# Single-head cross attention: one folded projection Wq·Wkᵀ in place of two, and context rows loaded one tile ahead

## The chip, the cores and the metric

One core of a Trainium2 chip runs the whole kernel. The metric is the device time of one execution in microseconds (us), lower is better. The kernel before took 2476.36 us (median of three runs, 2470.38 to 2479.93).

## The reference

The input x is 32 sequences of 32 tokens with 512 numbers each (1024 tokens in all), and ctx is 32 sequences of 257 rows with 512 numbers. Two layers of cross attention, self attention and a mixture of experts follow each other. Only the first block of layer 0 is touched:

```python
q = layernorm(x) @ Wq + bq          # (32, 32, 512)
k = ctx @ Wk + bk                   # (32, 257, 512)
v = ctx @ Wv + bv
sim  = einsum('bid,bjd->bij', q, k) * 512 ** -0.5
attn = softmax(sim)
x = x + einsum('bij,bjd->bid', attn, v)
```

The kernel never forms k or v. It uses q·(ctx Wk + bk)ᵀ = (q Wkᵀ)·ctxᵀ + q·bk. The row vector q Wkᵀ is called qp here, and q·bk, one number for each token, is the shift. The values are taken in the same way: attn·ctx first, then times Wv.

## The kernel before, in words

A product that needs full precision is done in three TensorE passes (`mm3`, L132 to L136): both operands are split into a high part, which the fast matmul type holds exactly, and a low part, and high·high, high·low and low·high are added in PSUM. ScalarE makes the high part, VectorE or GpSimd subtracts it from the original for the low part.

Work is cut into blocks (`with nc.Block()`), in which every engine has a program of its own. Engines wait for each other by semaphores inside a block, and all engines meet at its end. All large loads are issued by SyncE (SP) in the order of its program: an instruction that waits holds back every load behind it.

Around the change there are these blocks, in order:

1. **Opening** (L143): SP loads x (2 MB) and waits for it. GpSimd makes an identity and two masks.
2. **Layer norm** (`layer_norm("na")`, L186): statistics of eight tiles of 128 tokens (L221, L224), normalised rows (L248), transposes (L304), high and low parts xh (L280) and xl (L253). Beside it SP loads Wq, Wkᵀ and Wv (L321), and ScalarE and GpSimd split Wq (L326, L332).
3. **Projections** (L374): for each half of the tokens (512) four q jobs of 12 matmuls (x by Wq), whose bias ScalarE adds (L397) and whose low part VectorE makes (L415), then four k jobs of 12 matmuls (q by Wkᵀ, copied out at L418), then 32 matmuls of 2 columns (L450) for the shift. SP loads the three biases and the first transposed context, Wkᵀ and Wv are split.
4. **Attention loop** (L474): eight tiles of 128 tokens, which are four sequences each. TensorE's order is written out by hand. In one turn it runs `scores(n+1)` (L614, needs the transposed context `ct` of tile n+1), `turn_p(n)` (L623), `turn_a(n-1)` (L646), `p_ctx(n)` (L632 and L636, needs the context rows `cn` and `cl` of tile n) and `values(n-1)` (L134 to L136). There is one set of four `ct` buffers and one set of four `cn` buffers. So `ct` of a tile can be loaded only when the scores of the tile before are done, and `cn` only when `p_ctx` of the tile before is done.

Semaphore `s_sc` counts finished sequences of scores and starts with a credit of 8. `s_pv` counts finished sequences of p_ctx and starts with a credit of 4. The two load helpers wait like this before, and the SP loop calls them so:

```python
load_turned(n): eng.wait_ge(s_sc, SEQ * n + (SEQ + 1 + j))   # sequence j of scores(n-1) done
load_rows(n):   eng.wait_ge(s_pv, SEQ * n + SEQ)             # p_ctx(n-1) done
with eng.Fori(0, NT - 1) as n:
    load_turned(eng, n + 1)
    load_rows(n)
load_rows(NT - 1)
```

Of the kernel before, what the change touches and what calls it, by code (L numbers as in the profile page):

```python
# [16 lines left out]
F32 = mybir.dt.float32  # L17
# [71 lines left out]
def build(nc, d, out):  # L89
    with ExitStack() as ctx:  # L90
# [50 lines left out]

        s_x, s_id = sem("x_loaded"), sem("ident_made")
        with nc.Block() as block:  # L143
            @block.sync
            def _(eng):
                eng.dma_start(x[:], d["x"].rearrange("(t p) d -> p t d", p=P)).then_inc(s_x, 16)
                eng.wait_ge(s_x, 16)

            @block.gpsimd
            def _(eng):  # L150
                pool.memset(ident[:], 0.0).then_inc(s_id, 1)
                pool.memset(epst[:], LN_EPS)
                plain = Area(fa, F_SIZE).take(P)
                pool.memset(plain, 1.0).then_inc(s_id, 1)
                eng.wait_ge(s_id, 2)
                pool.affine_select(out=ident[:], in_=ident[:], compare_op=ALU.not_equal, fill=1.0,
                                   base=0, pattern=[[-1, P]], channel_multiplier=1)
                pool.tensor_copy(ones[:], plain)

                pool.affine_select(out=earlier[:], in_=plain, compare_op=ALU.is_gt, fill=0.0,  # L160
                                   base=0, pattern=[[1, P]], channel_multiplier=-1)
# [178 lines left out]
        def cross_one_head():  # L340
            scale = float(D) ** -0.5
            f, r = Area(fa, F_SIZE), Area(ra, R_SIZE)
            qp, bv, bk, bq, shift = f.take(DC, T), f.take(D), f.take(DC), f.take(DC), f.take(NT)
            f2 = f.at

            staging = [f.take(DC, D) for _ in range(3)]
            ct = [f.take(DC, S) for _ in range(SEQ)]
            f3 = f.at
            wv = r.take(DC, D), r.take(DC, D)
            bk_parts = r.take(DC, 2)  # L350
            r2 = r.at
            wq, wk = (r.take(DC, D), r.take(DC, D)), (r.take(DC, D), r.take(DC, D))
            q = [r.take(DC, HALF) for _ in range(2)]
# [4 lines left out]
            s_sc, s_bk = sem("xa_scores"), sem("xa_bk_split")  # L358

            def load_turned(eng, n):  # L360
                for j in range(SEQ):
# [5 lines left out]
            layer_norm("na", ahead=((load, high, low), (0, 1, 2), (0,)))  # L367
            s_b, s_mm, s_hi, s_out = sem("xa_biases"), sem("xa_product"), sem("xa_high"), sem("xa_taken")
# [3 lines left out]
            NB = 4  # L372

            with nc.Block() as block:  # L374
                @block.sync
                def _(eng):
# [3 lines left out]
                    load_turned(eng, 0)  # L380

                @block.gpsimd
                def _(eng):
                    low(eng, (1, 2))

                @block.scalar
                def _(eng):
                    high(eng, (1, 2))
                    eng.wait_ge(s_b, 48)
                    for j, (h, kind, c) in enumerate(jobs):  # L390
                        if kind != "q":
                            continue
                        eng.wait_ge(s_mm, j + 1)
                        if h:

                            eng.wait_ge(s_mm, len(jobs) // 2)
                        act.activation(q[0][:, c, :], banks[:, j % NB, :], ACT.Identity,  # L397
                                       bias=bq[:, c:c + 1]).then_inc(s_hi, 1)

                @block.vector  # L400
                def _(eng):
                    eng.wait_ge(s_b, 48)
                    eng.wait_ge(s_b, 48)
                    dve.tensor_copy(bk_parts[:, :, 0], bk).then_inc(s_bk, 1)
                    eng.wait_ge(s_bk, 1)
                    dve.tensor_tensor(bk_parts[:, :, 1], bk, bk_parts[:, :, 0].bitcast(F32),
                                      ALU.subtract).then_inc(s_bk, 1)
                    highs = 0
                    for j, (h, kind, c) in enumerate(jobs):
                        bank = banks[:, j % NB, :]  # L410
                        eng.wait_ge(s_mm, j + 1)
                        if kind == "q":
                            highs += 1
                            eng.wait_ge(s_hi, highs)
                            ins = dve.scalar_tensor_tensor(q[1][:, c, :], bank, bq[:, c:c + 1],  # L415
                                                           q[0][:, c, :].bitcast(F32), ALU.add, ALU.subtract)
                        elif kind == "k":
                            ins = dve.tensor_copy(qp[:, c, h * HALF:(h + 1) * HALF], bank)  # L418
                        else:
                            ins = dve.reduce_sum(shift[:, 4 * h:4 * h + 4],  # L420
                                                 bank[:, 0:8].rearrange("p (t k) -> p t k", k=2), AX_X)
                        ins.then_inc(s_out, 1)

                @block.tensor
                def _(eng):
                    for j, (h, kind, c) in enumerate(jobs):
# [5 lines left out]
                        if kind == "q":  # L432
                            eng.wait_ge(s_w[0], 1)
                            for k in range(DC):
                                ins = mm3(bank, wq[0][:, k, cols], wq[1][:, k, cols], xh[:, k, tok],
                                          xl[:, k, tok], k == 0, k == DC - 1)
                        elif kind == "k":
                            eng.wait_ge(s_w[1], 1)

                            eng.wait_ge(s_out, j - c)  # L440
                            for k in range(DC):
                                ins = mm3(bank, wk[0][:, k, cols], wk[1][:, k, cols], q[0][:, k, :],
                                          q[1][:, k, :], k == 0, k == DC - 1)
                        else:

                            eng.wait_ge(s_bk, 2)
                            for t in range(4):
                                for k in range(DC):
                                    for part in range(2):
                                        ins = pe.matmul(bank[:, 2 * t:2 * t + 2], q[part][:, k, t * P:(t + 1) * P],  # L450
                                                        bk_parts[:, k, :], start=(k + part == 0),
                                                        stop=(k == DC - 1 and part == 1))
# [3 lines left out]
            f = Area(fa, F_SIZE, f2)  # L456
            cn = [f.take(2, D) for _ in range(SEQ)]
            cl = f.take(D)
            f = Area(fa, F_SIZE, f3)
            r = Area(ra, R_SIZE, r2)  # L460
            qg = [f.take(DC, P) for _ in range(2)]
# [6 lines left out]
            s_ctx = [sem(f"xa_ctx{j}") for j in range(SEQ)]  # L468
            s_passed, s_cl, s_own, s_last = (sem(f"xa_{n}") for n in ("passed", "last_rows", "own", "p_last"))
            (s_qg, s_bias, s_exp, s_tp, s_pt, s_pv, s_a, s_at, s_ah, s_al, s_o, s_x, s_links) = (  # L470
                sem(f"xa_{n}") for n in ("q_tile", "bias", "exp", "p_turned", "p_kept", "pv", "a_kept",
                                         "a_turned", "a_high", "a_low", "out", "x_added", "links"))

            with nc.Block() as block:  # L474
                @block.sync
                def _(eng):
                    def load_rows(n):

                        eng.wait_ge(s_pv, SEQ * n + SEQ)
                        eng.dma_start(cl[0:SEQ, :], d["ctxLast"][bass.ds(SEQ * n, SEQ), :]).then_inc(s_cl, 16)  # L480
                        for j in range(SEQ):

                            eng.wait_ge(s_pv, SEQ * n + j + 1)
                            eng.dma_start(cn[j], d["ctx"][SEQ * n + j, 0:2 * P, :]
                                          .rearrange("(k p) e -> p k e", p=P)).then_inc(s_ctx[j], 16)
# [1604 lines left out]
def layouts(i):  # L2090
# [4 lines left out]
    def units(up1, up2, down):  # L2095
# [14 lines left out]
        "L0_xattn_WkT": t(i["L0_xattn_Wk"]),  # L2110
        "L0_attn_w_qkvT": t(i["L0_attn_w_qkv"]),
# [11 lines left out]
    for name in ("L0_xattn_Wq", "L0_xattn_bq", "L0_xattn_bk", "L0_xattn_Wv", "L0_xattn_bv", "L0_attn_ln_gamma",  # L2123
# [21 lines left out]
```

## Time and profile before

| what | value |
|---|---|
| timed runs, median (lowest to highest) | 2476.36 us (2470.38 to 2479.93) |
| profiled execution, span from the first to the last instruction | 2457.6 us |
| TensorE busy (matmul) | 2120.9 us, 86% |
| VectorE, ScalarE, GpSimd busy | 46%, 37%, 39% |
| mean granted TensorE clock | 0.922 |
| all transfers | 298.99 MB, mean 122 GB/s |

The profiled execution was listed with its span alone; the median of the timed runs lies 18.8 us above that span, which is taken as what lies around it.

In the views below PE is TensorE's matmul, PEld its weight load, DVE VectorE, ACT ScalarE, POOL GpSimd, SPq and PEq are the instruction queues of SyncE and TensorE. L12 is line 12 of the kernel. A row of the timeline has the start in us, the busy us, then engine, line, operation, output<-input, the count, and in brackets the idle time before it with what released it. A row of the windows has the stretch, its length, busy us and instruction count of each engine, the granted TensorE clock (1.00 is full speed), the busy share of the DMA engines and the GB/s moved.

### The profile page before, as it was taken

Reading aid. Unit: us, or ns where it says so; the run is one execution under the profiler, and the core shown is the slowest. Engines: PE = TensorE matmul, PEld = TensorE weight load, DVE = VectorE, ACT = ScalarE, POOL = GpSimd, SP = SyncE. Lnnn points to the kernel's source line nnn. Section 1 sums busy time; section 2 is a strip of 40 time slices with the busy share of each in tenths; the row PEclk is TensorE's granted clock in tenths of the full one; section 3 lists DMA queues with packets and bytes.
Section 4 is the critical chain, followed back from the end, with each engine's and each line's share of the span. In section 5 each row is a group of like instructions: output and inputs, shape, how many; then the busy total and the mean of one; then the engine's idle time right before and its main releaser. Section 6 shows DMA issues by size and latency. Waiting matters only on the chain. (4 is left out here: it accounts for less than half of the span.)

```text
span 2457.6 us, 37707 instructions
## 1 busy us (share of the span) xinstructions
PE 2120.9 (86%) x13252; PEld 1820.9 (74%) x13252; DVE 1130.6 (46%) x2057; ACT 897.9 (37%) x1479; POOL 950.9 (39%) x641
## 2 busy tenths in 40 slices
PE   6895888837999975999999999986765999999994
PEld 5543766637999963788888888865544999999993
DVE  4145463765555565232233222348664445544542
ACT  2112121215666642223232323223222555555551
POOL 2002312005777773232223222213212666666654
PEclk9996999958999987999999999968886999999997
DMA  3483000016888883011001100010003566656653
GB/s 124 169 313 115 18 23 29 1 35 245 274 283 276 282 277 128 18 30 33 26 26 28 33 26 26 18 48 5 22 6 142 200 217 213 209 199 219 214 192 124
DMA packets 102450, 298.99 MB, mean 122 GB/s; under 512 B 10912, under 2 KB 27936, under 8 KB 102336
## 3 DMA queue, kind: packets, MB, share of 16 engines
q1 hardware_dynamic: 76928, 232.88, 28.3%
q0 software_dynamic: 11840, 38.81, 5.2%
q10 hardware_dynamic: 13600, 26.22, 2.8%
q8 instruction: 51, 0.84, 0.1%
q14 instruction: 31, 0.25, 0.0%
HBM read 265.10 MB, written 32.77 MB: 121 GB/s over the span
## 5 line engine op out<-in xcount | busy, mean ns | idle before, releaser
L134 PE MATMUL banks<-ra 128*128 128x256 f32 (+3 forms) x3004 | 982.9, 327 | 55.9 <-DVE x L1040 24.7
L135 PE MATMUL banks<-ra 128*128 128x256 f32 (+3 forms) x3004 | 967.4, 322 | 0.0
L136 PE MATMUL banks<-ra 128*128 128x256 f32 (+3 forms) x3004 | 964.0, 321 | 0.0
L134 PEld LDWEIGHTS banks<-ra 128*128 128x128 f32 (+1 forms) x3004 | 577.9, 193 | 119.5 <-issue 39.5
L136 PEld LDWEIGHTS banks<-ra 128*128 128x128 f32 (+1 forms) x3004 | 577.7, 192 | 43.7
L135 PEld LDWEIGHTS banks<-ra 128*128 128x128 f32 (+1 forms) x3004 | 579.4, 193 | 36.1
L1475 POOL TENSOR_TENSOR ra<-fa,ra 128x1024 fp32r<-128x1024 f32 x187 | 445.9, 2385 | 235.3 <-ACT ra L1508 234.4
L1508 ACT ACTIVATE ra<-fa 128x1536 fp32r<-128x1536 f32 x190 | 281.5, 1482 | 85.1 <-DMA fa<-in_L_units 67.9
L1592 DVE TENSOR_TENSOR ra<-fa,ra 128x256 fp32r<-128x256 f32 x190 | 162.7, 856 | 92.0 <-ACT ra L1532 92.0
L332 POOL TENSOR_TENSOR ra<-fa,ra 128x2048 fp32r<-128x2048 f32 (+2 forms) x22 | 85.7, 3905 | 284.3 <-ACT ra L326 277.4
L1567 DVE TENSOR_TENSOR ra<-fa,ra 128x512 fp32r<-128x512 f32 x190 | 133.6, 703 | 114.9 <-ACT ra L1508 108.2
L1824 POOL TENSOR_TENSOR fa<-fa 128x1028 f32<-128x1028 f32 x32 | 60.9, 1902 | 284.0 <-DVE fa L1916 284.0
L1907 DVE TENSOR_TENSOR fa<-banks,fa 128x512 f32<-128x512 f32 x64 | 44.3, 692 | 269.6 <-PE banks L136 269.6
L1812 POOL TENSOR_TENSOR ra<-fa,ra 128x1032 fp32r<-128x1032 f32 x32 | 77.0, 2405 | 168.7 <-ACT ra L1843 168.7
L1590 DVE TENSOR_TENSOR fa<-banks,fa 128x256 f32<-128x256 f32 x190 | 80.5, 424 | 124.4 <-ACT fa L1528 124.4
L304 PE MATMUL banks<-ident,na 128*128 128x128 f32 x192 | 40.9, 384 | 109.9 <-DVE na L248 86.6
L1528 ACT ACTIVATE fa<-banks 128x256 f32<-128x256 f32 x190 | 72.7, 383 | 165.5 <-PE banks L136 165.4
L1470 POOL DMA_INDIRECT fa<-normed_scratch,fa x100 | 100.1, 1001 | 55.9 <-POOL fa L1465 40.7
L304 PEld LDWEIGHTS banks<-ident,na 128*128 128x128 f32 x192 | 33.4, 203 | 118.0 <-DVE na L248 89.9
L1532 ACT ACTIVATE ra<-fa 128x256 fp32r<-128x256 f32 x190 | 79.4, 418 | 112.5 <-DVE fa L1590 112.5
L1851 ACT ACTIVATE fa<-banks,fa 128x258 f32<-128x258 f32 x128 | 60.9, 477 | 148.5 <-PE banks L136 148.5
L1574 DVE TENSOR_TENSOR ra<-banks,ra 128x512 fp32r<-128x512 f32 x100 | 64.4, 687 | 108.9 <-ACT ra L1512 108.8
(222 smaller groups left out, 2608.4 us busy)
## 6 DMA issues: line engine op xcount, KB each, us to landing
fa<-in_L_units SPq DMA_DIRECT2D x190, 768.0 KB, 4.3
fa<-in_ctxT SPq DMA_DIRECT2D x64, 514.0 KB, 5.3
ea_y_scratch<-fa ACTq DMA_DIRECT2D x35, 512.0 KB, 4.5
fa<-in_ctx SPq DMA_DIRECT2D x32, 512.0 KB, 5.3
eb_y_scratch<-fa ACTq DMA_DIRECT2D x15, 512.0 KB, 3.7
fa<-in_L_attn_w_qkvT SPq DMA_DIRECT2D x6, 1024.0 KB, 6.2
normed_scratch<-na SPq DMA_DIRECT2D x16, 256.0 KB, 2.1
x<-in_x SPq DMA_DIRECT2D x1, 2048.0 KB, 8.2
```

Of the source, the lines that this page charges most:

```text
L134: pe.matmul(psum, lh, rh, start=first, stop=False)
L135: pe.matmul(psum, lh, rl, start=False, stop=False)
L136: return pe.matmul(psum, ll, rh, start=False, stop=last)
L332: pool.tensor_tensor(lo, staging[k % slots], hi.bitcast(F32), ALU.subtract).then_inc(s_w[k], 1)
L1470: pool.indirect_dma_start(xt[u][:, s, :], None, normed_dram, bass.IndirectOffsetOnAxis(ap=ids[u].bitcast(U32)[:, s:s + 1], axis=0)).then_i ...
L1475: pool.tensor_tensor(wl[b][:, 0:2, :], st[b][:, 0:2, :], wh[b][:, 0:2, :].bitcast(F32), ALU.subtract).then_inc(s_wp, 1)
L1508: act.activation(wh[b], st[b], ACT.Copy).then_inc(s_wh, 1)
L1532: act.activation(hh_[b], hf[b], ACT.Copy).then_inc(s_hh, 1)
L1567: dve.tensor_tensor(wl[b][:, 2, :], st[b][:, 2, :], wh[b][:, 2, :].bitcast(F32), ALU.subtract).then_inc(s_wd, 1)
L1590: dve.tensor_tensor(hf[b], banks[:, HB + b, CAP:2 * CAP], sg[b], ALU.mult).then_inc(s_hf, 1)
L1592: dve.tensor_tensor(hl[b], hf[b], hh_[b].bitcast(F32), ALU.subtract).then_inc(s_hl, 1)
L1812: pool.tensor_tensor(cx[u][1], stg[u], cx[u][0].bitcast(F32), ALU.subtract).then_inc(s_cl, 1)
```

## The change

The kernel forms M = Wq·Wkᵀ on the chip and multiplies x by M, so that q is never formed. The biases come in as vectors: u = Wq·bk gives the shift x·u, bq·Wkᵀ (`through_k`) is added to qp, and bq·bk (`both`) to the shift. The opening now loads Wqᵀ, Wkᵀ, x, Wv and the first transposed context, splits both weights, runs 48 matmuls for M and 72 matmuls of 2 columns for the bias terms, and takes the statistics of x. The layer norm block loads the first context rows and splits Wv. The projection block keeps the k jobs and the shift. The SP loop of the attention block calls the same two helpers, but with `load_rows(n + 1)`. `layer_norm`, `split_programs` and TensorE's program in the attention loop are the same text.

```diff
-        s_x, s_id = sem("x_loaded"), sem("ident_made")
-        with nc.Block() as block:
-            @block.sync
-            def _(eng):
-                eng.dma_start(x[:], d["x"].rearrange("(t p) d -> p t d", p=P)).then_inc(s_x, 16)
-                eng.wait_ge(s_x, 16)
...
-            load, high, low, s_w = split_programs("xa", [
-                (*wq, columns(d["L0_xattn_Wq"])), (*wk, columns(d["L0_xattn_WkT"])),
-                (*wv, columns(d["L0_xattn_Wv"]))], staging)
+            cn = [Area(fa, F_SIZE, f2 + 2 * D * j).take(2, D) for j in range(SEQ)]
+            load, high, low, s_w = split_programs("xa", [(*wv, columns(d["L0_xattn_Wv"]))], staging[2:])
...
-            layer_norm("na", ahead=((load, high, low), (0, 1, 2), (0,)))
+            def load_rows(eng, n):
+                if not (isinstance(n, int) and n == 0):
+                    eng.wait_ge(s_pv, SEQ * n + SEQ)
+                eng.dma_start(cl[0:SEQ, :], d["ctxLast"][bass.ds(SEQ * n, SEQ), :]).then_inc(s_cl, 16)
+                for j in range(SEQ):
+                    if not (isinstance(n, int) and n == 0):
+                        eng.wait_ge(s_pv, SEQ * n + j + 1)
+                    eng.dma_start(cn[j], d["ctx"][SEQ * n + j, 0:2 * P, :]
+                                  .rearrange("(k p) e -> p k e", p=P)).then_inc(s_ctx[j], 16)
             with nc.Block() as block:
                 @block.sync
+                def _(eng):
+                    eng.dma_start(staging[0], columns(d["L0_xattn_WqT"])).then_inc(s_wq, 16)
+                    eng.dma_start(staging[1], columns(d["L0_xattn_WkT"])).then_inc(s_wk, 16)
+                    eng.dma_start(x[:], d["x"].rearrange("(t p) d -> p t d", p=P)).then_inc(s_x, 16)
+                    load(eng)
+                    load_turned(eng, 0)
+                    eng.wait_ge(s_x, 16)
+                    eng.wait_ge(s_b, 48)
+                @block.gpsimd
...
+                    eng.wait_ge(s_wh, 1)
+                    pool.tensor_tensor(wq[1], staging[0], wq[0].bitcast(F32), ALU.subtract).then_inc(s_wlo, 1)
+                @block.scalar
                 def _(eng):
                     eng.dma_start(bq, d["L0_xattn_bq"]).then_inc(s_b, 16)
                     eng.dma_start(bk, d["L0_xattn_bk"]).then_inc(s_b, 16)
                     eng.dma_start(bv, d["L0_xattn_bv"].partition_broadcast(P)).then_inc(s_b, 16)
...
+                    eng.wait_ge(s_wq, 16)
+                    act.activation(wq[0], staging[0], ACT.Copy).then_inc(s_wh, 1)
+                    eng.wait_ge(s_wk, 16)
+                    act.activation(wk[0], staging[1], ACT.Copy).then_inc(s_wh, 1)
+                    for c in range(DC):
+                        eng.wait_ge(s_fold, c + 1)
+                        act.activation(m[0][:, c, :], banks[:, c, :], ACT.Copy).then_inc(s_mh, 1)
+                @block.vector
+                def _(eng):
...
+                    eng.wait_ge(s_wh, 2)
+                    dve.tensor_tensor(wk[1], staging[1], wk[0].bitcast(F32), ALU.subtract).then_inc(s_wlo, 1)
+                    eng.wait_ge(s_x, 16)
+                    for t in range(NT):
+                        dve.bn_stats(stats[:, t, :], x[:, t, :])
+                    for c in range(DC):
+                        eng.wait_ge(s_mh, c + 1)
+                        dve.tensor_tensor(m[1][:, c, :], banks[:, c, :], m[0][:, c, :].bitcast(F32),
+                                          ALU.subtract).then_inc(s_ml, 1)
...
+                @block.tensor
+                def _(eng):
+                    eng.wait_ge(s_wlo, 2)
+                    for c in range(DC):
+                        cols = slice(c * P, (c + 1) * P)
+                        for k in range(DC):
+                            ins = mm3(banks[:, c, :], wq[0][:, k, cols], wq[1][:, k, cols], wk[0][:, k, :], wk[1][:, k, :],
+                                      k == 0, k == DC - 1)
+                        ins.then_inc(s_fold, 1)
+                    eng.wait_ge(s_parts, 1)
+                    for w, parts, bank in ((wq, bk_parts, 4), (wk, bq_parts, 5)):
+                        for c in range(DC):
+                            for k in range(DC):
+                                for part in range(2):
+                                    ins = pe.matmul(banks[:, bank, 2 * c:2 * c + 2], w[part][:, k, c * P:(c + 1) * P],
+                                                    parts[:, k, :], start=k + part == 0, stop=k == DC - 1 and part == 1)
...
+                    for k in range(DC):
+                        for part in range(2):
+                            ins = pe.matmul(banks[:, 6, 0:2], bq_wide[part][:, k, :], bk_parts[:, k, :], start=k + part == 0,
+                                            stop=k == DC - 1 and part == 1)
+            made.add("statistics")
+            layer_norm("na", ahead=((load_first_rows, high, low), (0,), (0,)))
-            jobs = [(h, kind, c) for h in range(NHALF) for kind, c in
-                    [("q", c) for c in range(DC)] + [("k", c) for c in range(DC)] + [("shift", 0)]]
+            jobs = [(h, kind, c) for h in range(NHALF) for kind, c in [("k", c) for c in range(DC)] + [("shift", 0)]]
...
-                        elif kind == "k":
-                            ins = dve.tensor_copy(qp[:, c, h * HALF:(h + 1) * HALF], bank)
+                        if kind == "k":
+                            ins = dve.tensor_scalar(qp[:, c, h * HALF:(h + 1) * HALF], bank, through_k[:, c:c + 1], None,
+                                                    ALU.add)
...
-                                ins = mm3(bank, wk[0][:, k, cols], wk[1][:, k, cols], q[0][:, k, :],
-                                          q[1][:, k, :], k == 0, k == DC - 1)
+                                ins = mm3(bank, m[0][:, k, cols], m[1][:, k, cols], xh[:, k, tok], xl[:, k, tok],
+                                          k == 0, k == DC - 1)
...
                     with eng.Fori(0, NT - 1) as n:
                         load_turned(eng, n + 1)
-                        load_rows(n)
-                    load_rows(NT - 1)
+                        load_rows(eng, n + 1)
```

## Rows read from the trace of the kernel before

**Rows 1.** The page: span, busy time, and the KB of one transposed load.

```profile
span 2457.6 us, 37707 instructions
PE 2120.9 (86%) x13252; PEld 1820.9 (74%) x13252; DVE 1130.6 (46%) x2057; ACT 897.9 (37%) x1479; POOL 950.9 (39%) x641
...
fa<-in_ctxT SPq DMA_DIRECT2D x64, 514.0 KB, 5.3
```

**Rows 2.** Timeline, one steady turn of the attention loop: TensorE and SP's queue.

```profile
136.47 4.63 PE L614 MATMUL banks<-fa 128*32 128x257 f32 x32
...
138.57 3.03 SPq L365 DMA_DIRECT2D fa<-in_ctxT  x4
...
142.81 1.11 PE L632 MATMUL banks<-fa 4*128 4x512 f32 x2 [0.81 <-DVE fa L557]
...
143.86 1.94 PE L636 MATMUL banks<-fa 128*32 128x512 f32 x16
...
146.65 2.18 SPq L484 DMA_DIRECT2D fa<-in_ctx  x4
148.73 4.63 PE L614 MATMUL banks<-fa 128*32 128x257 f32 x32
```

**Rows 3.** Timeline: where p_ctx(0) and p_ctx(6) end, the loop's first and seventh.

```profile
106.86 3.20 PE L636 MATMUL banks<-fa 128*32 128x512 f32 x16
...
180.53 1.94 PE L636 MATMUL banks<-fa 128*32 128x512 f32 x16
```

**Rows 4.** Windows of 1 us around the end of a p_ctx at 145.8.

```profile
145.00:146.00 1.00, 1.00 (x9) 0.27 (x2) 0.02 (x1) 0.00 (x0) 0.00 (x0) 1.00 1.02 415
...
148.00:149.00 1.00, 1.00 (x6) 0.48 (x5) 0.16 (x1) 0.00 (x0) 0.00 (x0) 1.00 0.51 129
149.00:150.00 1.00, 1.00 (x8) 0.58 (x8) 0.86 (x2) 0.00 (x0) 0.00 (x0) 1.00 1.04 401
```

**Rows 5.** L484, 180 to 195 us: last rows issued at 184.4; issue to landing.

```profile
L484 SPq DMA_DIRECT2D fa<-in_ctx x4: 378/468/468, 183.0 to 184.4; - x4
...
DMA to landing us min/median/max: 3.9/5.2/6.3
```

**Rows 6.** Timeline: stretches of TensorE at the lower clock, and the projections' marks.

```profile
27.70 0.76 PE L134 MATMUL banks<-xh,ra 128*128 128x512 f32 x1 [4.64 <-PEq L186]
...
30.83 0.46 PE L135 MATMUL banks<-xl,ra 128*128 128x512 f32 x1
...
42.38 0.47 PE L134 MATMUL banks<-ra 128*128 128x512 f32 x1 [1.73 <-DVE ra L415]
...
53.34 3.63 PE L450 MATMUL banks<-ra 128*128 128x2 f32 x32
...
71.58 0.47 PE L134 MATMUL banks<-ra 128*128 128x512 f32 x1 [1.72 <-DVE ra L415]
...
88.00 6.72 PE L614 MATMUL banks<-fa 128*32 128x257 f32 x32 [1.34 <-ACT fa L508]
```

**Rows 7.** Windows of 1 us: in p_ctx(0), and in the next layer norm.

```profile
108.00:109.00 1.00, 1.00 (x8) 0.22 (x4) 0.00 (x0) 0.00 (x0) 0.00 (x0) 0.50 1.01 403
...
223.00:224.00 1.00, 0.61 (x3) 0.64 (x4) 1.00 (x2) 0.13 (x1) 1.00 (x1) 0.50 0.00 0
```

**Rows 8.** Timeline, opening and layer norm.

```profile
14.68 0.64 DVE L224 BATCH_NORM_AGGREGATE moments<-stats 128x2 f32<-128x6 f32 x8
...
18.44 0.69 DVE L253 TENSOR_TENSOR xl<-banks,xh 128x512 fp32r<-128x512 f32 x1
...
20.86 1.91 ACT L326 ACTIVATE ra<-fa 128x2048 fp32r<-128x2048 f32 x1
...
22.85 4.51 POOL L332 TENSOR_TENSOR ra<-fa,ra 128x2048 fp32r<-128x2048 f32 x1 [20.66 <-ACT ra L326]
...
34.37 4.62 DVE L406 TENSOR_TENSOR ra<-fa,ra 128x4 fp32r<-128x4 f32 x1
```

**Rows 9.** L321, first 27 us: landing of Wq, Wkᵀ and Wv after issue.

```profile
DMA to landing us min/median/max: 5.4/7.9/9.9
```

More of the change, by code:

```diff
@@ L343, in cross_one_head @@
             qp, bv, bk, bq, shift = f.take(DC, T), f.take(D), f.take(DC), f.take(DC), f.take(NT)
+            through_k, both, plain = f.take(DC), f.take(2), f.take(P)
             f2 = f.at
@@ L347, in cross_one_head @@
             ct = [f.take(DC, S) for _ in range(SEQ)]
+            cl = f.take(D)
             f3 = f.at
             wv = r.take(DC, D), r.take(DC, D)
-            bk_parts = r.take(DC, 2)
+            m = r.take(DC, D), r.take(DC, D)
+            bk_parts, bq_parts, u_parts = r.take(DC, 2), r.take(DC, 2), r.take(DC, 2)
             r2 = r.at
             wq, wk = (r.take(DC, D), r.take(DC, D)), (r.take(DC, D), r.take(DC, D))
-            q = [r.take(DC, HALF) for _ in range(2)]
-            load, high, low, s_w = split_programs("xa", [
-                (*wq, columns(d["L0_xattn_Wq"])), (*wk, columns(d["L0_xattn_WkT"])),
-                (*wv, columns(d["L0_xattn_Wv"]))], staging)
+            bq_wide = r.take(DC, P), r.take(DC, P)
+            cn = [Area(fa, F_SIZE, f2 + 2 * D * j).take(2, D) for j in range(SEQ)]
+            load, high, low, s_w = split_programs("xa", [(*wv, columns(d["L0_xattn_Wv"]))], staging[2:])
             s_ctxT = [sem(f"xa_ctxT{j}") for j in range(SEQ)]
-            s_sc, s_bk = sem("xa_scores"), sem("xa_bk_split")
+            s_ctx = [sem(f"xa_ctx{j}") for j in range(SEQ)]
+            s_cl, s_sc, s_pv = sem("xa_last_rows"), sem("xa_scores"), sem("xa_pv")
+            s_x, s_id, s_b, s_wq, s_wk = (sem(f"xa_{n}") for n in ("x_loaded", "ident_made", "biases", "wq_loaded", "wk_loaded"))
+            s_wh, s_wlo, s_parts, s_fold, s_mh, s_ml, s_u, s_links0 = (
+                sem(f"xa_{n}") for n in ("folded_high", "folded_low", "bias_parts", "folded", "m_high", "m_low", "u_split",
+                                         "links0"))
             def load_turned(eng, n):
@@ L379, in _ @@
                     eng.dma_start(bv, d["L0_xattn_bv"].partition_broadcast(P)).then_inc(s_b, 16)
[L380 to L398, printed above, removed]
+                    eng.wait_ge(s_wq, 16)
@@ new lines, in _ @@
+                    dve.tensor_tensor(bk_parts[:, :, 1], bk, bk_parts[:, :, 0].bitcast(F32), ALU.subtract)
+                    links.link(dve.tensor_tensor(bq_parts[:, :, 1], bq, bq_parts[:, :, 0].bitcast(F32), ALU.subtract))
+                    for part in range(2):
+                        ins = dve.tensor_copy(bq_wide[part], bq_parts[:, :, part].bitcast(F32).unsqueeze(2)
+                                              .to_broadcast([P, DC, P]))
+                    ins.then_inc(s_parts, 1)
@@ new lines, in _ @@
+                    dve.reduce_sum(through_k, banks[:, 5, 0:2 * DC].rearrange("p (c k) -> p c k", k=2), AX_X)
+                    dve.reduce_sum(both[:, 0:1], banks[:, 6, 0:2], AX_X)
+                @block.tensor
[14 more added lines that the diff above has]
+                                                    parts[:, k, :], start=k + part == 0, stop=k == DC - 1 and part == 1)
+                        if bank == 4:
+                            ins.then_inc(s_fold, 1)
+                    for k in range(DC):
+                        for part in range(2):
+                            ins = pe.matmul(banks[:, 6, 0:2], bq_wide[part][:, k, :], bk_parts[:, k, :], start=k + part == 0,
+                                            stop=k == DC - 1 and part == 1)
+                    ins.then_inc(s_fold, 1)
@@ L409, in _, with load_first_rows @@
+            made.add("statistics")
+            def load_first_rows(eng, _):
+                load_rows(eng, 0)
+            layer_norm("na", ahead=((load_first_rows, high, low), (0,), (0,)))
+            s_mm, s_out = sem("xa_product"), sem("xa_taken")
+            jobs = [(h, kind, c) for h in range(NHALF) for kind, c in [("k", c) for c in range(DC)] + [("shift", 0)]]
+            NB = 4
+            with nc.Block() as block:
+                @block.vector
+                def _(eng):
                     for j, (h, kind, c) in enumerate(jobs):
@@ L467, in cross_one_head @@
             at = [(r.take(DC, P), r.take(DC, P)) for _ in range(2)]
[L468 to L471, printed above, removed]
+            s_passed, s_own, s_last = (sem(f"xa_{n}") for n in ("passed", "own", "p_last"))
+            (s_qg, s_bias, s_exp, s_tp, s_pt, s_a, s_at, s_ah, s_al, s_o, s_x, s_links) = (
+                sem(f"xa_{n}") for n in ("q_tile", "bias", "exp", "p_turned", "p_kept", "a_kept",
                                          "a_turned", "a_high", "a_low", "out", "x_added", "links"))
@@ L476, in _ @@
                 def _(eng):
[L477 to L485, printed above, removed]
                     with eng.Fori(0, NT - 1) as n:
                         load_turned(eng, n + 1)
-                        load_rows(n)
-                    load_rows(NT - 1)
+                        load_rows(eng, n + 1)
                 @block.gpsimd
@@ L2122, in layouts @@
     }
-    for name in ("L0_xattn_Wq", "L0_xattn_bq", "L0_xattn_bk", "L0_xattn_Wv", "L0_xattn_bv", "L0_attn_ln_gamma",
+    for name in ("L0_xattn_bq", "L0_xattn_bk", "L0_xattn_Wv", "L0_xattn_bv", "L0_attn_ln_gamma",
                  "L0_attn_ln_beta", "L0_attn_b_out", "L0_ffn_gate_bias", "L1_xattn_W_Q", "L1_xattn_b_Q",
```

72 lines of the change are left out of this document (30 added, 42 removed).

## The prediction, made before the changed kernel ran

> **What bounds the kernel now.** The page comes first: TensorE's matmuls are busy for 2120.9 of 2457.6 us [rows 1], so any stage is suspected of being bound by TensorE until its own rows say otherwise. The timeline of the stage comes second, because the change touches only the first 205 us. It shows two kinds of stretch. Up to 88.0 us there are the opening, the layer norm and the projections, whose marks are in [rows 6, 8]. From there on the attention loop turns at an even pace: one `scores` starts at 136.47 and the next at 148.73, 12.26 us apart [rows 2]. In that turn TensorE runs scores (4.6 us), p_ctx (142.81 to 145.80) and values (until 148.7) with only about 1 us of idle time ahead of L632. It is TensorE's loop, but narrowly so, and the windows of 1 us say how narrowly: the DMA engines move 415 GB/s until 146, drop for about two microseconds and are back at 401 GB/s from 149 on [rows 4]. One turn brings in four transposed pieces of 526 KB (514 times 1024 bytes) and four pieces of rows of 524 KB [rows 1] (the second by its shape), 4.2 MB, which take 10.4 us at 405 GB/s (between the two rates of [rows 4]). So 10.4 of 12.26 us are filled with transfers, and this works only because the two sets are requested at different moments: `ct` from 138.57 on, as each sequence of scores ends, and the rows after p_ctx, at 146.65 [rows 2].
>
> **Part 1, the order of the loads in the loop (costs).** Both helpers wait as before for their own index, but SP now runs `load_turned(n+1)`, `load_rows(n+1)`. The wait in `load_rows(n+1)` is `s_pv >= 4(n+1)+4`, with a credit of 4: it passes when p_ctx(n) is done. Behind it in SP's program stands `load_turned(n+2)`, which needs only scores(n+1). Before, `load_rows(n)` stood there, and it waited for p_ctx(n-1), which was long past when scores(n+1) ended. TensorE's order is scores(n+1), ..., p_ctx(n), values(n-1), scores(n+2). The rows are requested at the same moment as before (p_ctx done), but `ct` for the next scores moves from the end of scores(n+1) to behind the rows, with one `values` of 2.9 us to hide in. All 4.2 MB must then flow between the end of p_ctx(n) and the last quarter of scores(n+2).
>
> How long that takes, counted from the end of p_ctx at 145.80: the transfers are back at full rate at about 148.7 (129 GB/s in 148 to 149 is a third of a microsecond at 405) [rows 4], so +2.9. Rows of 2.10 MB take 5.2 us, each piece of `ct` 1.3 us. A piece counts as landed about 0.6 us after its flow ends: the last rows of the loop were issued at 184.4 and took 6.3 us, to 190.7 [rows 5], and their flow ended at about 190.1. So `ct` lands at +10.0, +11.3, +12.6 and +13.9. TensorE is done with values at +2.9 (148.73) and stands idle for 7 us. A sequence of scores takes 1.16 us (4.63 / 4), so scores(n+2) ends at +15.05, and from there to the end of the next p_ctx it is 4.70 us (136.47 + 4.63 = 141.10 to 143.86 + 1.94 = 145.80) [rows 2]. One turn: 19.8 us.
>
> The clock adds to this. After 4.6 us idle, TensorE came back at the lower of its two levels (1.2 instead of 2.4 GHz) from 27.70 to about 30.8; at 88.0, after the columns of width 2, thirty-two passes of scores took 6.72 us instead of 4.63 [rows 6, 2]. If the first two sequences of a turn run at half speed (1.7 us each), scores ends at +15.75 instead of +15.05. If the drop falls on p_ctx as well, its sixteen passes of L636 cost what they did in p_ctx(0), 3.20 us instead of 1.94 [rows 3, 2], with the clock at 0.50 [rows 7], and L632 somewhat more. I take 0.7, nearer to the end that the pace of the landing `ct` hides: a turn of 20.5 us. The ends are 19.8 and 22.
>
> How many turns: scores(2) to scores(7) stand behind the new wait, which are six; `ct` of tiles 0 and 1 is requested as before, and after p_ctx(6) there is no scores left. Those six turns took 72.4 us before, from 110.06 to 182.47 [rows 3]. After: 6 x 20.5 = 123.0. The loop loses 50.6 us (46.4 to 59.6). Having the rows of tile 0 in advance gives nothing: p_ctx waits for VectorE's copy of p (L632, released by L557) [rows 2], and rows of a later tile still wait for p_ctx.
>
> **Part 2, the projections (gains).** Gone are eight q jobs of 12 matmuls and two waits for q's low part: 27.70 to 42.38, and the same piece of the second half, 71.58 minus 56.97 (53.34 + 3.63): 14.7 + 14.6 = 29.3 us [rows 6]. The added vector in L418's place hides under a job of 12 matmuls. What remains, k and shift, took 42.38 to 56.97 and 71.58 to 86.7, 29.7 us. The slow clock that sat in the q jobs does not go with them: it follows idling and the narrow matmuls, and takes about 1.4 us (3.1 us at half speed) in each half, so the block takes 29.7 + 2.8 + 1.3 (to 88.0) = 33.8 us instead of 60.3.
>
> **Part 3, the opening (costs).** Before, the layer norm's L224 starts at 14.68 and the first projection at 27.70, 13.0 us later [rows 6, 8]. Now L224 waits for the end of a block that holds the folding. Wqᵀ is issued first, at 0.8, and lands 5.4 us later, Wkᵀ at 9.1 [rows 9] (7.9 us after an issue 0.4 us later); the bias loads on ScalarE's queue may take up to 2 us of that. High part 1.91 us: 8.1; low part on GpSimd 4.51 us: 12.6 [rows 8]. VectorE's low part of Wkᵀ is ready to start at 11.0. Four times the 0.7 us of a low part of 512 gives 2.8 us, an estimate from L253 [rows 8]. L406, on 4 columns, took 4.62 us while GpSimd was subtracting [rows 8], so I let VectorE wait until 12.6: 15.4. Then 48 matmuls of 512 take 11.0 us (42.38 to 53.34) and 1.4 for the lower clock [rows 6]: 27.8. Seventy-two narrow matmuls at 3.63 / 32 = 0.113 us are 8.2 us; if the clock falls within them (it was low at 88.0, behind thirty-two of them), up to 11; I take 10: 37.8. VectorE's last sums and the end of the block: 38.6. The statistics of x (8 tiles) and the low parts of M lie under the matmuls. The 13.0 us of the layer norm follow, and I allow 0.6, an estimate, for the table load of ScalarE that the statistics used to hide: 52.2. Wv's split takes the place of Wq's, same sizes. So 24.5 us later than 27.7, with ends at 20 (no waiting, no clock drop) and 27.5.
>
> The Trainium skill's page "SBUF — State Buffer", section "Who interferes with whom", says that a VectorE operation with two inputs in SBUF and a GpSimd operation that reads SBUF exclude each other for the whole instruction. L406 agrees with it. Without the rule the opening would be 1.6 us shorter.
>
> Parts 2 and 3 together: scores(0) starts at 52.2 + 33.8 = 86.0 instead of 88.0, a gain of 2.0 us (ends: a gain of 6.5, a loss of 3). From scores(0) to the end of p_ctx(0) nothing changes, and nothing after the loop does.
>
> **The sum.** Against the profiled span: 2457.6 - 2.0 + 50.6 = 2506.2 us. The median of the runs lies 18.8 above that span, so 2525 us. With the lower ends 2476.4 - 6.5 + 46.4 = 2516, with the upper 2476.4 + 3 + 59.6 = 2539.
>
> **The rivals.**
> - *The lower clock stays for the whole loop.* Idle for 7 of 20 us in each turn, TensorE may never get back to 2.4 GHz, as in the next layer norm, where the row at 223 shows 0.50 with TensorE busy on and off [rows 7]. Four sequences of scores then take 6.9 us from +10.0, and the tail 4.7 + 1.7 for p_ctx + 0.5 for the turns of p and a (estimates from the ratio 3.20 to 1.94): a turn of 23.8 us, 142.8 for six, a loss of 70.4, and 2545 us. Against it: scores(0), begun at the low clock, lost only 2.1 us, so full speed was back after 4.2 us [rows 6, 2]. In one sentence of its own: the Trainium skill, page "TensorE: Matmul & The Clock Gate", section "HAM oscillation — how this bites in real kernels", says that a loop which waits for a transfer in every turn starts each turn at the low clock; by it every turn carries a slow piece, between my 20.5 and this 23.8, and the trace agrees as far as 27.70 goes.
> - *The transfer is hidden anyway, not slower.* The place is TensorE's wait at L614 for `ct` of tile n+2. It costs nothing if the request does not stand behind p_ctx(n), that is, if I count the credit of `s_pv` wrongly by one p_ctx; then the rows are requested a turn ahead of what I say, and the turn stays 12.26. It decides from +2.9: if `ct` has landed by then, all that is left is the opening's gain of 2.0, 2474 us, or 2470 at its better end. For it: the fold removes 29 us and puts back 24. Against it: the one set of `cn` buffers is read by p_ctx(n), so a wait for that p_ctx must be there, and 4.2 MB would have to flow in some 3 us.
>
> **Chances.** Forecast 0.77, lower clock 0.14, hidden transfer 0.09. The predicted time is the forecast's, 2525 us. The range reaches down to 2509, for a loop whose transfers flow a little better than in [rows 4] beside the spread of the runs, and up to 2548, which takes in the first rival. Under 0.5% (12 us) a difference can hardly be told from none. Slower by more: forecast and first rival, 0.91. The hidden transfer gives 2474, within 0.5% in most of its cases: 0.06, and 0.03 for faster.
>
> **What would show it.** In the loop: SP's issues of `ct` right behind the rows, after p_ctx; TensorE's wait before scores named after a DMA of in_ctxT, about 7 us in each of six turns; turns of 20 to 21 us; DMA engines idle from the end of scores to the next p_ctx. In the opening: folding from about 15 to 28 us, L224's successor at 38 to 39, scores(0) at 86. The prediction is wrong if turns stay near 12.3 us, or if scores(0) starts more than 7 us away from 86.

## The result, and the profile after

The changed kernel took 2533.45 us (median of 4 runs, 2524.2 to 2540.3), the kernel before 2473.37 us. The ratio is 1.0246, 95% interval 1.0214 to 1.0277: 60 us slower, where 48.6 were forecast (50.6 in the loop less 2.0 in the opening). The range (2509 to 2548) holds the time.

The views answer the steps in order. First the timeline of the loop after (start, busy us, engine, line; what ended the idle time). `scores` is now L654, `p_ctx` L676; SP issues `ct` at L350, the rows at L361.

```profile
105.90 3.66 PE L676 MATMUL banks<-fa 128*32 128x512 f32 x16
...
129.89 1.95 PE L676 MATMUL banks<-fa 128*32 128x512 f32 x16
...
132.52 1.93 SPq L361 DMA_DIRECT2D fa<-in_ctx  x4
...
135.01 2.14 SPq L350 DMA_DIRECT2D fa<-in_ctxT  x4
...
142.05 6.50 PE L654 MATMUL banks<-fa 128*32 128x257 f32 x32 [7.21 <-DMA fa<-in_ctxT]
...
151.25 1.95 PE L676 MATMUL banks<-fa 128*32 128x512 f32 x16
...
236.47 1.95 PE L676 MATMUL banks<-fa 128*32 128x512 f32 x16
```

The seven p_ctx from 109.56 to 238.42 bound six turns of 21.5 us, 128.9 us instead of 72.4 [rows 3]. Both sets of loads now go out behind p_ctx, which ends at 131.84: the rows at 132.5 and `ct` at 135.0, 3.2 us after it. Before, `ct` went out at 138.57, 7.2 us ahead of the end of that turn's p_ctx at 145.80 [rows 2]. TensorE then waits 7.21 us for a transfer. It waits 7.0 to 7.2 us in five of the six turns and 10.1 in the first, which has no `values` to run meanwhile. The waits of the loop sum this up (who waited for whom, total us, times, longest):

```profile
PEld banks L654 <- DMA fa<-in_ctxT: 49.9, 7, 11.9
PE banks L654 <- DMA fa<-in_ctxT: 47.2, 7, 10.1
```

The windows of 1 us of the same turn (TensorE, weight load, VectorE, ScalarE, GpSimd, clock, DMA share, GB/s), which answer [rows 4]:

```profile
134.00:135.00 1.00, 0.84 (x4) 0.36 (x2) 0.12 (x1) 0.00 (x0) 0.00 (x0) 1.00 0.50 162
135.00:136.00 1.00, 0.00 (x0) 0.00 (x0) 0.86 (x2) 0.00 (x0) 0.00 (x0) 1.00 1.01 389
...
140.00:141.00 1.00, 0.00 (x0) 0.00 (x0) 0.00 (x0) 0.00 (x0) 0.00 (x0) 0.50 1.01 401
...
143.00:144.00 1.00, 1.00 (x5) 0.45 (x5) 0.00 (x0) 0.00 (x0) 0.00 (x0) 0.50 1.04 419
...
145.00:146.00 1.00, 1.00 (x8) 0.44 (x6) 0.00 (x0) 0.00 (x0) 0.00 (x0) 0.50 0.17 58
146.00:147.00 1.00, 1.00 (x12) 0.58 (x10) 0.00 (x0) 0.00 (x0) 0.00 (x0) 0.99 0.00 0
```

The flow fills 134.7 to 145.2, 2.9 to 13.3 us after p_ctx. The clock column drops to 0.50 (1.2 GHz) between 139 and 140, while TensorE idles, and stays there for the first 4 us of scores. Last, the opening and projections, which answer [rows 6, 8]:

```profile
15.72 0.79 PE L134 MATMUL banks<-ra 128*128 128x512 f32 x1 [15.72 <-DVE ra L418]
...
28.61 9.31 PE L452 MATMUL banks<-ra 128*128 128x2 f32 x64
...
37.78 1.84 PE L458 MATMUL banks<-ra 128*128 128x2 f32 x8
...
53.17 0.47 PE L134 MATMUL banks<-xh,ra 128*128 128x512 f32 x1 [3.94 <-PEq L165]
...
88.67 5.92 PE L654 MATMUL banks<-fa 128*32 128x257 f32 x32 [1.61 <-ACT fa L548]
```

scores(0) starts at 88.67; it was 88.00, and 90.64 in a second execution of the kernel before (e7).

**The account between the two profiles.** Spans are 2529.7 and 2457.6, 72.1 us apart. To the end of p_ctx(0): 109.56 against 110.06, -0.5. Six turns: +56.5. From p_ctx(6) to the next layer norm (264.13 and 205.62): 25.7 against 23.15, +2.6. That is 58.5 us, close to the 60 of the medians. The other 13.6 lie in stages with the same text, above all in one wait of SP in the expert stage: before, after, and in a second execution of the kernel before (e7).

```profile
SPq L1427 <- DMA ea_y_scratch<-fa: 26.4, 1, 26.4
```
```profile
SPq L1467 <- DMA ea_y_scratch<-fa: 44.6, 1, 44.6
```
```profile
SPq L1427 <- DMA ea_y_scratch<-fa: 44.5, 1, 44.5
```

### The profile page after: what moved, and what is told of

It reads as the page before. It is cut to its first block and busy times, and to the rows that moved or that the text cites. A ratio compares the mean times of both kernels' runs of the same rounds, so it can differ in the third digit from the quotient of the medians.

```text
span 2529.7 us, 37651 instructions
## 1 busy us (share of the span) xinstructions
PE 2142.1 (85%) x13276; PEld 1831.1 (72%) x13276; DVE 1128.5 (45%) x2065; ACT 895.8 (35%) x1476; POOL 944.0 (37%) x640
## 5 line engine op out<-in xcount | busy, mean ns | idle before, releaser
L134 PE MATMUL banks<-ra 128*128 128x256 f32 (+3 forms) x2988 | 980.3, 328 | 72.4 <-DVE x L1080 25.3
L311 POOL TENSOR_TENSOR ra<-fa,ra 128x2048 fp32r<-128x2048 f32 (+2 forms) x20 | 75.5, 3789 | 352.7 <-ACT ra L305 346.1
L134 PE MATMUL banks<-xh,ra 128*128 128x512 f32 x224 | 94.6, 422 | 17.5 <-PEq L165 16.4
```

What stands on the lines that cost most here:

```text
L134: pe.matmul(psum, lh, rh, start=first, stop=False)
L311: pool.tensor_tensor(lo, staging[k % slots], hi.bitcast(F32), ALU.subtract).then_inc(s_w[k], 1)
```

## The experiments

Ratios are to the kernel before, run beside each on the same chip.

**e1: the changed kernel, order of loads as before.**

```diff
-                        load_turned(eng, n + 1)
-                        load_rows(eng, n + 1)
+                    load_turned(eng, 1)
+                    with eng.Fori(0, NT - 2) as n:
+                        load_turned(eng, n + 2)
+                        load_rows(eng, n + 1)
+                    load_rows(eng, NT - 1)
```

> The changed kernel with one thing undone: SP issues the context rows of tile n+1 behind the transposed context of tile n+2, as before the change (the first rows are still loaded in the layer norm). Theory A (the loop's loss is the position of ct behind the rows in SP's queue): turns of p_ctx come back from 21.4 us to 12.2, the wait of scores for in_ctxT falls from 47 us to under 5, total 57 us below the changed kernel, so within 0.5% of the kernel before (about 2475). Rival B (the loop is slower because of something else that changed, buffers at other addresses or the first rows loaded early): turns stay above 15 us and the total stays above 2500.

Measured 2469.92 us, ratio 0.9995 (0.9978 to 1.0013). The timeline:

```profile
132.31 1.95 PE L678 MATMUL banks<-fa 128*32 128x512 f32 x16
...
144.59 1.95 PE L678 MATMUL banks<-fa 128*32 128x512 f32 x16
```

12.28 us a turn, and only 1.5 us of waiting for in_ctxT. The whole loss is the order, within the 4 us of the interval. The run also shows the folding without the new order in the loop: no gain and no loss within the same 4 us.

**e2: the kernel before, new order alone.**

```diff
+                    load_rows(0)
                     with eng.Fori(0, NT - 1) as n:
                         load_turned(eng, n + 1)
-                        load_rows(n)
-                    load_rows(NT - 1)
+                        load_rows(n + 1)
```

> The kernel before with nothing but the new order of loads: rows of tile 0 at the start of the loop block, then ct(n+1), rows(n+1). Theory A: six turns of about 21.4 us instead of 12.2, +55 us against before, about 2530; the opening and the projections as before (scores(0) at 88). Rival B: under +10 us, because both projections and the folding are needed for the loss.

Measured 2520.45 us, ratio 1.0193 (1.0167 to 1.0218). The timeline:

```profile
125.73 1.94 PE L636 MATMUL banks<-fa 128*32 128x512 f32 x16
...
137.47 6.11 PE L614 MATMUL banks<-fa 128*32 128x257 f32 x32 [6.80 <-DMA fa<-in_ctxT]
...
146.27 1.94 PE L636 MATMUL banks<-fa 128*32 128x512 f32 x16
```

The same stall without any folding. Five turns from 127.67 to 233.52 average 21.2 us, and with the one ahead of them the six turns take 54.1 us more than before. Rival B falls. The ratio is worth 48 us, less than the 60 of the changed kernel, but the two intervals touch (1.0218 and 1.0214), so no run shows that the rest of the change costs anything.

**e3: work for TensorE inside the stall.**

```diff
+                        if not isinstance(n, int):
+                            for _ in range(28):
+                                pe.matmul(banks[:, u, :], wv[0][:, 0, 0:P], wv[0][:, 1, :], start=True, stop=True)
                         for j in range(SEQ):
                             eng.wait_ge(s_ctxT[j], 16 * n + 16)
```

> The changed kernel with 28 extra matmuls of 512 columns (their result is overwritten, nothing uses it) put ahead of the wait for ct in each of the six scores of the loop, some 6 us of work inside a stall of 7. Theory C (the part of a turn above 19.8 us is the lower clock of scores after the stall): scores take 4.6 to 5.5 us instead of 5.9 to 7.4, turns fall from 21.4 to about 20, total 6 to 10 us below the changed kernel. Rival D (the scores are slow because ct lands late, one piece after the other): scores still spread over 5.9 to 7.4 us, total the same within 3 us; if the extra matmuls outlast the stall it gets slower by that.

Measured 2524.08 us, ratio 1.0219 (1.0188 to 1.0249), against 1.0246 for the changed kernel: lower, but the intervals overlap, so the verdict rests on the timeline.

```profile
94.92 1.90 PE L657 MATMUL banks<-fa 128*32 128x257 f32 x8 [1.35 <-DMA fa<-in_ctxT]
...
150.08 1.95 PE L679 MATMUL banks<-fa 128*32 128x512 f32 x16
...
162.09 5.73 PE L657 MATMUL banks<-fa 128*32 128x257 f32 x32 [0.67 <-DMA fa<-in_ctxT]
...
170.59 1.95 PE L679 MATMUL banks<-fa 128*32 128x512 f32 x16
```

All six scores take 5.72 to 5.75 us, where the changed kernel's took 7.39, 6.50, 6.10, 5.89, 7.41 and 6.61, 6.65 on average. The granted clock is now 1.00 through the wait and the scores (150 to 171). So 0.9 us a turn is the low clock. What stays above 4.63 us is the pace of the landing pieces, rival D's share. Turns average 20.4 us (131.77 to 233.95, five of them). The turn ahead of these gained nothing (22.3 us in both kernels): its scores were faster too, but its p_ctx ran at the low clock and took 3.64 us.

**e4: half of the rows' bytes.** Tiles 1 to 7 leave out the second half of their rows, so the kernel's result is not the reference's.

```diff
-                    eng.dma_start(cn[j], d["ctx"][SEQ * n + j, 0:2 * P, :]
-                                  .rearrange("(k p) e -> p k e", p=P)).then_inc(s_ctx[j], 16)
...
+                        eng.dma_start(cn[j][:, 0, :], d["ctx"][SEQ * n + j, 0:P, :]).then_inc(s_ctx[j], 16)
```

> The changed kernel with half of the context rows loaded for tiles 1 to 7 (the other half of each buffer keeps old data): 1.05 MB less in front of ct in each of six turns. Theory A (scores wait for ct behind the rows, at some 405 GB/s): ct lands 2.6 us earlier and each turn is 2.6 us shorter (21.4 to 18.8), total about 16 us below the changed kernel. Rival E (the turn is set by latency and waits, not by bytes): under 5 us.

Measured 2524.39 us, ratio 1.0223 (1.0188 to 1.0258). The timeline:

```profile
137.81 6.04 PE L657 MATMUL banks<-fa 128*32 128x257 f32 x32 [4.79 <-DMA fa<-in_ctxT]
...
146.55 1.95 PE L679 MATMUL banks<-fa 128*32 128x512 f32 x16
```

The wait shrinks from 7.2 to 4.8 us in this turn and by 2.3 us on average, where the bytes left out take 2.6 us at 405 GB/s. The six turns average 19.3 us and take 13 us less than the changed kernel's. The bytes in front of `ct` set the wait, as theory A says. By the ratios the total fell by only 6 us, where 16 were expected; each ratio has an interval of 8 us or more on either side, so the totals settle nothing here, and the reading rests on the timeline.

**e5: the rows on GpSimd's queue.** `load_rows(eng, n + 1)` moved from SP's program to GpSimd's, with semaphores of its own.

> The changed kernel with the rows of tiles 1 to 7 issued by GpSimd instead of SP, with the same waits, so that SP holds only ct. Theory A (what hurts is that ct's request stands behind an instruction that waits for p_ctx): turns back at 12 to 13 us, total within 0.5% of the kernel before. Rival F (the order of the bytes matters, whoever issues them): turns stay above 18 us.

Measured 2486.78 us, ratio 1.0065 (1.0034 to 1.0096). Neither theory fits exactly: no more stall for `ct`, but a small one for the rows.

```profile
PEld banks L680 <- DMA fa<-in_ctx: 10.3, 8, 2.5
...
PE banks L680 <- DMA fa<-in_ctx: 4.1, 5, 1.6
...
PE banks L657 <- DMA fa<-in_ctxT: 2.0, 2, 1.4
```

Six turns from 110.23 to 195.24 average 14.2 us. So of the 9.2 us that a turn of the changed kernel loses, 7.3 are the wait in front of `ct` in one program. The remaining 2 us are not even: three turns are back at 12.2 to 12.5 us, the others take 17.5, 15.8 and 14.7. In the first of these rows and `ct` were issued at the same time (111.9 and 112.1), and the rows took 9.1 us to land (median), where they took 5.3 in e1. So the order of the bytes, rival F, seems to have a small share. Issuing may have one as well (four loads take GpSimd 2.84 us, SP 1.93). No run separates the two.

**e6: e1, with the folding inside the layer norm's block.** TensorE folds ahead of the transposes (banks 4 to 7), the narrow matmuls follow them. `extra[0]` holds the 48 matmuls of M, `extra[1]` the 72 narrow ones.

```diff
                     eng.sem_inc(s_turned, L)
+                    if extra:
+                        extra[0](eng)
...
                             ins.then_inc(s_turned, 1)
+                    if extra:
+                        extra[1](eng, s_lo)
```

> As e1, and the folding moved from the opening into the layer norm's block: the 48 matmuls ahead of the transposes in PSUM banks 4 to 7, the 72 narrow ones behind them, statistics of x in the same block. If the opening's cost is that folding and layer norm stand one behind the other (block after block), the first projection starts at about 47 to 48 us instead of 53.3 and the total is 5 us below e1. If the layer norm's own work is held up by the folding as much as it saves (VectorE and ScalarE wait for transposes behind 12.7 us of matmuls), the projection starts at 52 to 54 and the total equals e1.

Measured 2466.37 us, ratio 0.9974 (0.996 to 0.9989). The timeline:

```profile
17.09 0.77 PE L134 MATMUL banks<-ra 128*128 128x512 f32 x1 [17.09 <-PEq L375]
...
35.20 12.22 PE L462 MATMUL banks<-ra 128*128 128x2 f32 x64
...
49.78 0.77 PE L134 MATMUL banks<-xh,ra 128*128 128x512 f32 x1 [0.65 <-PEq L165]
```

The projections start at 49.8 instead of 53.2 (e1), less than hoped. Part of the reason is that the 64 narrow matmuls now take 12.2 us instead of 9.6 (e1): the clock is at 0.50 from 38 us on. The total is 5 us below e1's, as expected, but the two intervals overlap (up to 0.9989, from 0.9978).

**e8: e6 without the term q·bk.** It adds one number to a whole row of scores, and softmax cancels it. Wq·bk, bq·bk and both groups of shift matmuls are gone.

```diff
-            jobs = [(h, kind, c) for h in range(NHALF) for kind, c in [("k", c) for c in range(DC)] + [("shift", 0)]]
+            jobs = [(h, kind, c) for h in range(NHALF) for kind, c in [("k", c) for c in range(DC)]]
...
-                        links.link(dve.tensor_tensor(top[:, u:u + 1], mx[:, u:u + 1], sh, ALU.add))
-                        dve.tensor_scalar(bias[:, u:u + 1], top[:, u:u + 1], sh, -scale, ALU.subtract,
-                                          ALU.mult).then_inc(s_bias, 1)
+                        dve.tensor_scalar(bias[:, u:u + 1], mx[:, u:u + 1], -scale, None, ALU.mult).then_inc(s_bias, 1)
```

> As e6, without the term q.bk, which is one number for a whole row of scores and cancels in the softmax: gone are 40 of the 72 narrow matmuls of the folding and both groups of 32 behind the projections. If the narrow matmuls cost what they take (0.11 to 0.17 us each, 104 of them, some 14 us, with the lower clock they leave behind), scores(0) starts at about 70 us instead of 84.5 and the total is 12 to 16 us below e6, about 2453. If the clock drops anyway because of other idling, the gain is under 9 us.

Measured 2442.02 us, ratio 0.9886 (0.9859 to 0.9913), faster than both kernels. The timeline:

```profile
42.61 0.77 PE L134 MATMUL banks<-xh,ra 128*128 128x512 f32 x1 [0.51 <-PEq L165]
...
69.22 4.62 PE L650 MATMUL banks<-fa 128*32 128x257 f32 x32 [1.95 <-ACT fa L547]
```

scores(0) starts at 69.2 instead of 84.5 (e6), and runs at full clock (4.62 us, not 6.25). It gained more than expected: 0.0088 of 2469 us is 22 us against e6. The two traces show 20.8 of them ahead of the next layer norm (183.62 and 204.40). Of these, 17.4 lie ahead of the end of p_ctx(0): 15.3 before scores(0) and most of the rest in it. In the six turns another 3.5 us are gained. 1.7 of those are one p_ctx that ran at the low clock in e6. The rest is a steady gain that the expectation left out: without the added term VectorE is done sooner, TensorE waits 0.4 us instead of 0.8 ahead of `p_ctx`'s first matmul, and a turn takes 11.9 us instead of 12.2.

**e9: the kernel before without q·bk**, two projections kept.

> The kernel before with two projections, without the term q.bk: both groups of 32 narrow matmuls are gone, nothing is folded. If e8's 25 us come from the shift alone, this kernel is as fast as e8 (ratio to before 0.989) and the folding is worth nothing even when it is hidden. If the narrow matmuls take only their 7.7 us and 3 to 4 us of lower clock behind them, it is 10 to 12 us faster than before (ratio 0.9955), and the folded kernel e8 keeps a lead of some 15 us, since it drops 104 narrow matmuls and 48 wide ones against these 64.

Measured 2451.27 us, ratio 0.9954 (0.9937 to 0.997). The term is worth 11 us in the old form. Between 0.9954 and 0.9886 lie 17 us, give or take 8, for folding that is hidden and carries no q·bk; at the next layer norm e8's trace is 11.5 us ahead of e9's (183.62 and 195.12).

**e7: the kernel before once more**, for a second trace (one execution).

> The kernel before, for a second trace of it. The profile of before waited 26.4 us at L1427 for the store of ea_y_scratch, in the expert stage that the change does not touch, all later ones 44.7. If that is a difference between executions, the wait here is 44.7 and the span is near 2470. If the change causes it, the wait is 26.4 again.

2480.4 us, span 2478.6, the wait 44.5 us. So the 18 us in that wait are a difference between executions, and the profile of before was a lucky one. e9's trace has the short wait as well (26.6 us). From the next layer norm to the end these two take 2252 and 2254 us, all the other traces, with the long wait, 2261 to 2269. What makes the store late stays open, and so does how often it is: e9's profiled execution lies at the median of its six.

The second trace also shows how much the stages around the change vary with the same kernel:

```profile
90.64 6.66 PE L614 MATMUL banks<-fa 128*32 128x257 f32 x32 [1.34 <-ACT fa L508]
...
193.01 4.62 PE L636 MATMUL banks<-fa 128*32 128x512 f32 x16
```

scores(0) starts 2.6 us later than in the first trace, the last p_ctx takes 4.62 us instead of 3.02, and the next layer norm comes at 210.77 instead of 205.62. Against this trace the changed kernel is 53 us behind at that mark, against the first 58.5.

## Why the prediction was right, point by point

- **The order of the loads.** Right in mechanism and place: requests, a wait of 7 us (10 in the first of the six turns), the flow from +2.9 to +13.3. e1 shows that the order is the whole loss, e2 that it needs no folding, e5 that most of it is the wait in front of `ct` in SP's program. The term was too small: 50.6 us forecast, 56.5 measured. First `ct` landed at +10.2 (+10.0), and the tail from scores to the end of p_ctx took 4.65 (4.70). The mis-sized term is scores: 5.75 us forecast, 6.65 measured on average, times six is 5.4. Two causes. I priced the last sequence at 1.16 us, a quarter of an unbroken run, but a sequence that runs alone takes 1.90 us at full clock (e3's row at 94.92). Three pieces 1.28 us apart and a last sequence of 1.90 give 5.74 us, which is what e3's scores take. The trace of before had this at 95.67, in a row that I did not use:

```profile
95.67 1.90 PE L614 MATMUL banks<-fa 128*32 128x257 f32 x8 [0.95 <-DMA fa<-in_ctxT]
```

  And the low clock cost 0.9 us a turn, not 0.7 (e3, five of six turns).
- **The rival with the low clock throughout** (23.8 us a turn) did not come: the clock was back before p_ctx in each of the six turns, whose p_ctx took 1.95 us. The granted clock stood at 0.50 when scores began in every one of them, and that cost 0.9 of 21.5 us. The Trainium skill, page "TensorE: Matmul & The Clock Gate", section "HAM oscillation — how this bites in real kernels", named the right effect, a slow start after each wait.
- **The hidden transfer** fell: `ct` landed 7 us late.
- **The opening.** Folding began at 15.7 (15.4), ended at 28.8 (27.8), the narrow matmuls at 39.6 (37.8), the projections began at 53.2 (52.2). Right within a microsecond or two, but the start of the folding was right in part by luck. The exclusion of VectorE by GpSimd, priced at 1.6 us, was not where I put it: the high part of Wkᵀ was only done at 12.83, because its load landed 1.8 us later than forecast, and GpSimd was done at 12.3, before that. VectorE was held up elsewhere, if it was, in a cast of 4 columns that ended with GpSimd's subtraction and took 2.55 us, where the next cast of the same shape took 0.16. This cast reads one operand, so it is not the two-input case that I had named, and that it waited for GpSimd is inferred from the two ends:

```profile
8.49 3.81 POOL L390 TENSOR_TENSOR ra<-fa,ra 128x2048 fp32r<-128x2048 f32 x1 [6.30 <-ACT ra L398]
9.77 2.55 DVE L409 CAST ra<-fa 128x4 fp32r<-128x4 f32 x1 [9.77 <-DMA fa<-in_L_xattn_bv]
```

- **The projections.** 35.5 us, 33.8 forecast. In sum scores(0) came 0.7 us later instead of 2.0 earlier. But e7 has it at 90.64 for the kernel before, so two executions of one kernel differ here by more than the forecast gain, and the term can't be told from zero. e1 confirms in whole runs that the algebra is worth nothing in this form (0.9995). One bound was added up wrongly: the slow end of the opening, 27.5 us later instead of 24.5, makes a loss of 1 us for scores(0), not 3, which takes 2 us off the upper end of 2539 and nothing off the forecast.
- **Outside the loop and the opening** I expected no difference. From scores(0) to the end of p_ctx(0) it was 1.2 us less, from p_ctx(6) to the next layer norm 2.6 more, where the last p_ctx took 4.67 us instead of 3.02. e7 has 4.62 there without the change. With 5.9 us too little in the loop and 2.7 in the opening this is the whole distance from 48.6 to the 58.5 of the traces: every miss but the 1.2 went the same way, and the range was wide enough to hold them.
- **The time around the span.** I took the 18.8 us between span and median for what lies around the span. It is not: the changed kernel's execution of 2531.49 us has a span of 2529.7, 1.8 us less. The profile of before was simply 14 us faster than the median of 2473.37. The forecast was not harmed, because the two steps, from the median to the span and back, cancel.

## What to carry to other kernels

A load that waits for a late event holds back every load behind it in the same program, even those whose own condition was met long ago: order the issues by the moment each becomes possible, and count for each what stands in front. In a loop whose transfers fill 85% of a turn, moving one request from 7 us ahead of the end of p_ctx to 3 us behind it cost 9 us in every turn. Work taken out in algebra gains only if what is put in its place overlaps something: the fold alone gave 0.9995, and moved into the next block 0.9974, a step as small as its interval. Look for terms that cancel: q·bk, which softmax cancels, was worth 11 us in the old form and 22 in the folded one, against 6 for the fold with the term kept.

## What the runs showed of the hardware that I had not expected

During matmuls of 2 columns with full 128x128 weights the granted clock fell although the profile shows TensorE busy throughout: in the changed kernel's opening it stood at 1.00 for the first 4.3 us of them, then at 0.55 and 0.50. Windows over those three stretches, columns as above:

```profile
28.60:32.90 4.30, 4.30 (x41) 4.29 (x39) 1.19 (x4) 0.60 (x1) 0.00 (x0) 1.00 0.01 4
32.90:37.70 4.80, 4.80 (x27) 4.80 (x26) 0.00 (x0) 0.00 (x0) 0.00 (x0) 0.55 0.00 0
37.70:39.60 1.90, 1.90 (x10) 1.84 (x9) 0.00 (x0) 0.00 (x0) 0.00 (x0) 0.50 0.00 0
```

The low clock reaches into the wide matmuls that follow. In e6 these begin 0.65 us after the narrow ones, and their first 4 us ran at 0.50. In the kernel before, the narrow group at 53.34 still ran at 1.00, and the clock was at 0.50 from 58.3 to 61.3, in wide matmuls behind it, with TensorE busy all the time. That the narrow matmuls are the cause is borne out by e8 and e9, which have none ahead of scores(0) in the projections: there scores(0) took 4.62 and 4.63 us, against 6.25 in e6 and 6.72 before.
